# Scan stage: the product with V goes behind the next scores, and VectorE's normalisation one slot on

## What is computed

```python
scores = jnp.einsum('bqkgd,bskd->bkgqs', Qg, K) / scale
scores = jnp.where(causal, -jnp.inf, scores)
attn = jax.nn.softmax(scores, axis=-1)
out = jnp.einsum('bkgqs,bskd->bqkgd', attn, V).reshape(Bx, Tx, C)
...
def step(state, inp):                       # over 512 time steps
    d, b, c, u = inp
    dA = jnp.exp(d[..., None] * A)          # 512 channels x 16 states
    state = state * dA + (d * u)[..., None] * b[:, None, :]
    y = jnp.einsum('bdn,bn->bd', state, c)
    return (state, y)
```

## Time and profile before

| | us |
|---|---|
| median of 3 runs (1241.05 to 1241.61) | 1241.31 |
| the profiled execution, whole | 1238.74 |
| its span, first to last instruction | 1236.9 |
| of it the stage `mix`, first top to last normalisation | 171.3 to 700.5 |

### The profile page before, as it was taken

How to read it: one execution, slowest core, us unless ns; L and a number is a source line. 1 busy time by engine, 2 the same in 40 slices (tenths; PEclk the granted TensorE clock), 3 DMA queues, 4 the chain that set the end, 5 groups by cost and what they waited for, 6 DMA issues and landing times. The chain is left out here.

```text
span 1236.9 us, 18614 instructions
## 1 busy us (share of the span) xinstructions
PE 1073.2 (87%) x6368; PEld 642.0 (52%) x6368; DVE 806.6 (65%) x1195; ACT 668.3 (54%) x1438; POOL 673.2 (54%) x587
## 2 busy tenths in 40 slices
PE   7999838888888888888888899999999989999970
PEld 3444325555555555555555444444444457676740
DVE  5477779999999999999999476631760013333327
ACT  3566768889888888898888424202010012223220
POOL 1033369999999999999999630202041124444430
PEclk9999959999999999999999999999999999999995
DMA  6210001101111111111331212103027314333219
GB/s 204 87 36 19 18 18 35 35 28 35 35 36 32 30 35 36 36 33 63 95 102 45 90 48 103 69 34 116 20 79 244 102 44 128 127 128 129 77 49 385
DMA packets 51820, 94.74 MB, mean 77 GB/s; under 512 B 9806, under 2 KB 17998, under 8 KB 51728
## 3 DMA queue, kind: packets, MB, share of 16 engines
q1 hardware_dynamic: 44208, 72.82, 17.9%
q0 software_dynamic: 7520, 20.72, 5.4%
HBM read 74.51 MB, written 20.84 MB: 77 GB/s over the span
## 5 line engine op out<-in xcount | busy, mean ns | idle before, releaser
L604 POOL TENSOR_TENSOR w_all<-w_all 128x512 f32<-128x512 f32 x256 | 321.1, 1275 | 0.6 <-POOLq L96 0.3
L778 DVE TENSOR_TENSOR_SCAN w_all<-da,w_all 128x512 f32<-128x512 f32 x256 | 298.0, 1206 | 0.0
L712 ACT ACTIVATE da<-w_all,a_flat 128x512 f32<-128x512 f32 x256 | 179.6, 702 | 9.0 <-PEq L96 7.7
L683 PE MATMUL yb<-ident,w_all 128*128 128x128 f32 x1024 | 161.6, 281 | 7.5 <-DVE acc L786 7.5
L633 PE MATMUL sc<-w_all,attn 32*128 32x384 f32 (+3 forms) x512 | 105.0, 486 | 45.5 <-ACT w_all L720 22.8
L720 ACT ACTIVATE w_all<-sc,neg_max 128x128 f32<-128x128 f32 (+3 forms) x256 | 134.1, 539 | 16.5 <-DVE neg_max L770 15.5
L659 PE MATMUL ob<-w_all,v 128*32 128x128 f32 x1280 | 94.7, 277 | 52.8 <-ACT w_all L729 52.8
L683 PEld LDWEIGHTS yb<-ident,w_all 128*128 128x128 f32 x1024 | 113.5, 141 | 37.0 <-issue 30.6
L770 DVE TENSOR_REDUCE neg_max<-sc 128x2 f32<-128x256 f32 (+3 forms) x128 | 104.2, 814 | 34.2 <-PE sc L636 34.2
L1166 POOL TENSOR_TENSOR w_all<-w_all 128x512 f32<-128x512 f32 x24 | 29.4, 1226 | 165.0 <-ACT w_all L1337 165.0
L729 ACT ACTIVATE w_all<-tb 128x256 f32<-128x256 f32 (+2 forms) x192 | 102.8, 535 | 29.7 <-PE tb L648 29.7
(11 more groups left out here) (199 smaller groups left out, 1630.6 us busy)
## 6 DMA issues: line engine op xcount, KB each, us to landing
w_all<-b_scratch SPq DMA_DIRECT2D x64, 256.0 KB, 3.3
w_all<-in_w_up SPq DMA_DIRECT2D x16, 512.0 KB, 6.0
w_all<-in_w_down SPq DMA_DIRECT2D x16, 512.0 KB, 6.8
w_all<-sorted_y SPq DMA_DIRECT2D x16, 512.0 KB, 10.3
attn<-in_x SPq DMA_DIRECT2D x4, 1024.0 KB, 6.8
w_all<-in_x SPq DMA_DIRECT2D x16, 256.0 KB, 4.1
norms<-attn SPq DMA_DIRECT2D x4, 1024.0 KB, 4.3
out_dram<-acc SPq DMA_DIRECT2D x16, 256.0 KB, 8.9
```

The lines of the kernel that those rows point to most:

```text
L604: pool.tensor_tensor(dbu[:, k, :], keep["du"][i // N][:, k * T:(k + 1) * T], b_all[i % 2][:, :], ALU.mult).then_inc(pool_dbu.sem, pool_dbu ...
L683: last = pe.transpose(yb[which][:, k * P:(k + 1) * P], state[i % 2][:, k, t * P:(t + 1) * P], ident[:, :])
L712: act.activation(da[unit % 2][:, :], keep["dt"][i // N][:, k * T:(k + 1) * T], ACT.Exp, scale=keep["a_flat"][:, unit % (N * KD):unit % (N ...
L778: dve.tensor_tensor_scan(state[i % 2][:, k, :], da[unit % 2][:, :], dbu[:, k, :], 0.0, ALU.mult, ALU.add).then_inc(dve_scan.sem, dve_scan. ...
```

## The change

TensorE's W(g-3) is taken from the head of the slot and put behind SC(g+1), ahead of P1 (and in slot 2 ahead of P0). VectorE's normalisation of a quad moves from the end of slot 2 to slot 3, between scan 1 and scan 2. VectorE's loop gets one more, otherwise empty, slot for the last normalisation, and the reciprocal is kept from running in it. Nothing is added or removed, and no tile changes.

```diff
             for g in range(UNITS + 3):
+                if 0 <= g - 2 < UNITS:
+                    turn_state(g - 2, 0)
+                if spread_in(g) is not None:
+                    spread(spread_in(g))
+                elif 0 <= g - 2 < UNITS:
+                    turn_prob(g - 2, 0)
+                if 0 <= g - 2 < UNITS:
+                    turn_state(g - 2, 1)
+                if g + 1 < UNITS:
+                    scores(g + 1)
                 if 0 <= g - 3 < UNITS:
                     weigh_v(g - 3)
-                if 0 <= g - 2 < UNITS:
-                    turn_state(g - 2, 0)
-                    if spread_in(g) is not None:
-                        spread(spread_in(g))
-                    else:
-                        turn_prob(g - 2, 0)
-                    turn_state(g - 2, 1)
-                elif spread_in(g) is not None:
-                    spread(spread_in(g))
-                if g + 1 < UNITS:
-                    scores(g + 1)
                 if 0 <= g - 2 < UNITS and spread_in(g) is not None:
                     turn_prob(g - 2, 0)
                 if 0 <= g - 2 < UNITS and (g - 2) % NT >= 2:
@@
-            for g in range(UNITS + 3):
-                if g % 8 == 0 and g >= 8:
+            for g in range(UNITS + 4):
+                if g % 8 == 0 and 8 <= g <= UNITS:
@@
                 if g < UNITS:
                     top(g)
                     scan(2 * g)
+                if spread_in(g - 1) is not None:
+                    normalize(spread_in(g - 1))
+                if g < UNITS:
                     scan(2 * g + 1)
                 if 0 <= g - 2 < UNITS:
                     weigh_c(g - 2)
-                if spread_in(g) is not None:
-                    normalize(spread_in(g))
```

## The result

The changed kernel takes **1257.2 us** (median of 4 runs, 1256.4 to 1259.1) beside 1241.2 for the kernel before: +16.0 us, ratio 1.0135 with a 95% interval of 1.0117 to 1.0153. The forecast was +6.9 us, 1248.2, with a range up to 1255. The sign was right and the size less than half of the measured one.

The account below looks back on a forecast made before the run. It took the chain from SC to SC, through E and TensorE's arrival, as bound, with VectorE fullest. Terms of +4.0, +3.9 and -1.0 gave +6.9 us on the median of 1241.31: 1248.2 us, range 1235 to 1255.

Parts of the forecast that it names:

- The rooms and the delays: SC starts 0.50 to 1.45 us later than E allows in four slots; moved W delays E by 0.59 to 0.96 us.
- The price of a W with its switch: W ahead of the transposes costs 0.055 us a record plus 0.12 us for the switch.
- The normalisation: In slot 3 between the scans it costs 0; without cover from the late E(3), 0.6 us a quad, 9 us in all.
- The end of the stage: In the last slots, without SC, W stands beside ScalarE's copy of R: at most one W of 16 records, -1.0 us.
- The waits: TensorE's before W almost gone; ScalarE's before line 729 from 26.1 to some 60 to 70 us; VectorE newly waits for decays.
- The lower bound: W between SC and P1 costs only its record pitch, no switch: quad -0.64 us, about -10 us in all, 1231.
- the sum: Over all quads, +4.0 for SC(6) and SC(7), +3.9 for the slots behind R, -1.0 at the end: +6.9 us.
- upper bound: W costs its whole duration, 0.07 us more at each of five places: 0.35 us a quad, +5.5, 1254; range up to 1255.
- The first (rooms win): W's delays to T1 and T0 are smaller, so rooms win: some 1235, at the full 1197; chance 0.20.
- the second (no change): Delays are some 0.1 us smaller, so rooms and delays cancel: 1241 us; chance 0.13.
- The third rival: VectorE's waits for d2 outlast its slack before top, 0.5 us each, three a quad: 1258; chance 0.07 with the fourth.
- The fourth: SC doesn't come earlier relative to E, so the table's fourth row isn't won: 1257; chance 0.07 with the third.

Follow-up runs that it names:

- experiment 1: The changed kernel run again with no edit: 1252.96 us, ratio 1.0112 to the kernel before on the same chip.
- experiment 4: Against the changed kernel, only TensorE's part kept, normalisation back at the end of slot 2: 1285.1 us. Only VectorE's part kept, TensorE's order as before: 1301.0 us.
- filled kernel: Changed kernel with the S1 transposes issued twice in slots 3, 4, 6 and 7: 1248.1 us; again beside the changed kernel on one chip, 1249.31 against 1258.27 us.

## Why the prediction fell short

**Point by point.** *The rooms and the delays* were right. The intervals from SC to SC at full clock, before, as forecast, and as the profile of experiment 1 shows them:

| | before | forecast | measured |
|---|---|---|---|
| SC(5) to SC(6) | 4.19 | 4.06 | 4.06 |
| SC(6) to SC(7) | 4.50 | 4.88 | 4.92 |
| SC(1) to SC(2) | 4.20 | 4.07 | 4.06 |
| SC(2) to SC(3) | 5.44 | 4.87 | 4.92 |
| SC(3) to SC(4) | 4.14 | 5.10 | 5.13 |
| the other three | 10.12 | 10.12 | 10.12 |
| quad | 32.59 | 33.10 | 33.21 |

The price of a W with its switch was right too (0.56, 0.78 and 1.00 us from W to the transposes behind it), and the sign of the change turned on it. The +0.62 a quad instead of +0.51 is three intervals that came out 0.03 to 0.05 us longer than worked out, 1.8 us over the stage. From SC(3)'s mask to E(3) it is 319.33 - 316.75 = 2.58 us (2.5 forecast).

*The normalisation* cost nothing in its new place, as forecast, and saved 0.60 us a quad that its old place would have cost behind the moved W (experiment 4). That W would find it done was right only because W is behind SC(4).

*The end of the stage*: -1.0 forecast, -0.9 measured.

*The waits*: TensorE's ahead of W gone, ScalarE's ahead of line 728 at 72 us with the falls and 64 in the filled kernel without them (60 to 70 forecast), VectorE's new waits for decays 19.0 us; the intervals above leave no room for a price of theirs.

*The lower bound*: with the delays of 0.37, 0.66 and 0.74 us that I gave, a quad changes by -0.59 us and not by -0.64; the 1231 stays.

*The step that failed* is the sum, which had no term for TensorE's clock. I read 1.00 in one quad of the kernel before and took it over to another order of the same work. In its place the runs show 1.0 us for each fall of the clock right behind SC(7): eight of them, 8.1 us, in the profiled execution, and 7.6 to 9.0 us between the changed kernel and its filled sister. With the clock held by the fill, the change costs 7.3 and 9.7 us against the kernel before on two chips, where the forecast was 6.9. So the mechanism and, within 3 us, its size stand, and the missing term is the other half of the loss. My upper bound, 1255, was drawn around the price of W alone; nothing in it allowed for a clock that the rows of before showed as constant.

*The rivals.* The first (rooms win) fell, and with it the second (no change): the delays arrive. Of its full result, 1197, I said that ScalarE's order forbids it. That holds for this change, but W behind P1 reaches 1200.2 without touching ScalarE's order. By the Trainium skill (Perfetto Trace Analysis, Identifying Performance Opportunities) the gaps of the most-contended engine are to be closed by making what they wait for start sooner or finish faster. The runs agree with it (VectorE busy 29.74 of 30.14 us with W last) once the whole chain behind VectorE's gaps is followed: SC waits for E, and E for P1. The third rival (VectorE's waits for d2 are added, 1258) fell with the intervals, which are 0.05 us longer than the chain's at most and not 0.5. The fourth (SC(3) wins nothing, 1257) fell too: SC(2) to SC(3) went from 5.44 to 4.92 us. That both name nearly the measured time is chance. What makes the second half of the loss is no rival that I had.

**What stays open** is what exactly lets the clock fall. Shown: filling four or five waits of TensorE in each quad removes the falls behind the first quad, in three profiles on three chips. Not settled: whether the wait ahead of SC(7) alone does it. The kernel with d2 ahead of T1 points the same way: it still waits 0.79 us ahead of SC(4), but only 0.19 ahead of SC(7), and its profile has no fall behind the first quad.

## What to carry to other kernels

In an engine that works in order, moving an operation past another takes its wait from those behind and gives its length to those that it now stands ahead of: list who waits for each of them, up to the loop's own recurrence, before and after. Here the best place was neither the head nor behind the scores but the very end of the slot, behind everything that another engine waits for, and it was worth 39 us where the place between cost 16. And a move that changes where TensorE idles wants a term for its clock, even where the profile before shows full clock in every repeat of the loop; issuing in the waits some work twice, with the same result, is a cheap way to measure that term.

## What the runs showed of the hardware

The granted clock of TensorE fell to 1.2 GHz for 3.4 us in a stage in which TensorE was busy 85% of the time and in which its longest wait in the slots ahead was 0.80 us. The kernel before, with 84% and waits of 0.7 to 1.0 us at other places, did not show it behind the first slots in its one profile. In three profiles of the changed kernel the falls come four in a row, each at the same place in the quad, right behind SC(7), and in other quads in other executions. A fall made W of 16 records 1.92 us long instead of 1.07, and cost 1.0 us in all. Adding 1.8 us of transposes to a quad of 33.2 us made the whole kernel 9.0 us faster on the same chip (median of four executions each). In TensorE's order a W of 8, 12 or 16 records ahead of 128x128 transposes took 0.56, 0.78 and 1.00 us to their start.
